# Edge loop of a graph attention layer: bf16 parts at register addresses, selection on VectorE, four message places

## The reference

```
src = randint(100000, 0, 6250); dst = sort((6250 * uniform ** 2))
h = (layernorm(x) @ W.T).reshape(n, 8, 32)
alpha = sum(h[src] * a_src) + sum(h[dst] * a_dst)
alpha += sum(relu(edge_attr @ edge_W.T + edge_b) * h[dst])     # per edge and head
alpha = where(alpha >= 0, alpha, 0.2 * alpha)
attn = softmax of alpha over the edges of one dst
out = segment_sum(h[src] * attn, dst) + bias;  x = x + out
x = x + experts(layernorm(layernorm(x)))                        # router, top 2, gelu
```

## Time and profile before

| | us |
|---|---|
| median of 3 runs (2123.89 to 2133.44) | 2126.27 |
| profiled execution | 2128.02 |
| its span | 2126.0 |
| PE busy | 2009.7 |
| DVE busy | 1515.8 |
| ACT busy | 1352.4 |
| POOL busy | 1181.9 |

### The profile page before, as it was taken

How to read it: one execution, slowest core, us unless ns; L and a number is a source line. 1 busy time by engine, 2 the same in 40 slices (tenths; PEclk the granted TensorE clock), 3 DMA queues, 4 the chain that set the end, 5 groups by cost and what they waited for, 6 DMA issues and landing times. The chain is left out here.

```text
span 2126.0 us, 41064 instructions
## 1 busy us (share of the span) xinstructions
PE 2009.7 (95%) x11612; PEld 1585.9 (75%) x11612; DVE 1515.8 (71%) x3458; ACT 1352.4 (64%) x3892; POOL 1181.9 (56%) x1125
## 2 busy tenths in 40 slices
PE   7799999999999999999999676899999999999997
PEld 6566666766666666666666434899999999999996
DVE  7289999999999999999999897544444444444442
ACT  4698888988988988988988565433333333333332
POOL 1377777776776766666666000355555555555553
PEclk9899999999999999999999887999999999999998
DMA  9766565555555555555554688222222222222221
GB/s 252 227 194 175 170 186 175 172 179 165 169 176 163 167 170 163 158 168 160 157 165 143 230 267 190 46 39 36 38 39 36 38 38 36 38 38 36 38 38 23
DMA packets 160559, 270.94 MB, mean 127 GB/s; under 512 B 36239, under 2 KB 114864, under 8 KB 160211
## 3 DMA queue, kind: packets, MB, share of 16 engines
q0 software_dynamic: 61920, 139.45, 27.6%
q1 hardware_dynamic: 89706, 121.22, 18.6%
q10 hardware_dynamic: 8712, 7.65, 1.1%
HBM read 231.06 MB, written 37.17 MB: 126 GB/s over the span
## 5 line engine op out<-in xcount | busy, mean ns | idle before, releaser
L679 POOL DMA_INDIRECT arena<-h_tab,src x784 | 759.6, 969 | 375.6 <-issue 211.8
L1687 ACT ACTIVATE arena<-psum,arena 128x128 f32<-128x128 f32 x840 | 240.1, 368 | 518.2 <-PE psum L1637 518.2
L881 PE MATMUL psum<-arena 128*128 128x256 f32 x1760 | 479.1, 395 | 9.9 <-DVE arena L973 8.0
L902 PE MATMUL psum<-arena 128*128 128x264 f32 x1760 | 475.0, 393 | 2.5 <-DVE arena L996 2.4
L1637 PEld LDWEIGHTS psum<-arena 128*128 128x128 f32 x3360 | 392.9, 192 | 7.5 <-issue 2.2
L902 PEld LDWEIGHTS psum<-arena 128*128 128x128 f32 x1760 | 320.4, 190 | 100.3 <-issue 50.8
L1637 PE MATMUL psum<-arena 128*128 128x128 f32 x3360 | 393.4, 276 | 1.8 <-DVE arena L1709 1.8
L881 PEld LDWEIGHTS psum<-arena 128*128 128x128 f32 x1760 | 318.8, 191 | 98.2 <-issue 42.5
L1653 PE MATMUL psum<-arena 128*128 x1680 | 379.8, 379 | 0.0
L1599 POOL DMA_INDIRECT out_rows<-arena,src x105 | 208.3, 1984 | 247.2 <-DVE arena L1722 244.2
L1653 PEld LDWEIGHTS psum<-arena 128*128 128x128 f32 x1680 | 311.1, 190 | 38.0
(11 more groups left out here) (233 smaller groups left out, 1917.9 us busy)
## 6 DMA issues: line engine op xcount, KB each, us to landing
arena<-rel_list SPq DMA_DIRECT2D x110, 512.0 KB
arena<-in_W SPq DMA_DIRECT2D x16, 1024.0 KB, 12.3
arena<-h_tab,src POOLq DMA_INDIRECT x784
arena<-ea_slots SPq DMA_DIRECT2D x440, 27.0 KB
arena<-in_x SPq DMA_DIRECT2D x12, 896.0 KB, 8.5
h_tab<-arena SPq DMA_DIRECT2D x6, 952.0 KB, 7.9
out_rows<-arena SPq DMA_DIRECT2D x5, 896.0 KB, 5.4
xn<-arena ACTq DMA_DIRECT2D x5, 896.0 KB, 6.9
```

The source lines that it names most:

```text
L679: pool.indirect_dma_start(rows[:, (p % RING * U + k) * TW:(p % RING * U + k + 1) * TW], None, d.h_tab[:, :], bass.IndirectOffsetOnAxis(ap= ...
L881: last = nc.tensor.matmul(ps[:, HDT + x, y * UE:(y + 1) * UE], hj[:, (s // 2 * 2 + y) % HJ, x * P:(x + 1) * P], oht[:, half % OT, (u + y) ...
L902: last = nc.tensor.matmul(ps[:, AGG + a % 2, 0:HS], oh[:, a % OH, k, :], msg[:, a % MSG, k, :], start=(k == 0), stop=(k == U - 1))
L1687: last = nc.scalar.activation(hT[:, b, h * P:(h + 1) * P], ps[:, UP + 2 * b + half, h % 4 * P:(h % 4 + 1) * P], ACT.Gelu, bias=b1_now[:, b ...
```

## The change

- `expand` multiplies in bf16: h of every node tile is kept in three bf16 parts that add up to the fp32 value (`PARTS` = 3), and PE takes its weights at a register address from there. The one-hot targets become bf16 (`d.rel`, `oht`). `node_rows` on ACT and its ring `hj` are gone.
- The parts are made in `prepare`: POOL for groups 0 to 5, four operations each, after its list gathers; DVE for group 6, in steps 2 to 5 of the loop. h itself passes through three stage buffers, and the sums of a node tile lie over parts that have been used: `acc` shares the arena with them. ACT clears two tiles' places at a time, four times a round, behind the expansion (`clear_ahead`), in place of all at the start.
- DVE makes all selections.
- `MSG` is 4.
- Arena addresses move. W1 is loaded in halves: four at the loop's end, five in `attend`, seven in `route`; all of W2 is loaded in `attend`, three experts at its start and the others behind the groups whose sums are used up.

Core of the diff (the arena's bookkeeping and the moved loads are left out):

```diff
-RING, RENC, HJ, OH, OT, EB, MSG = 18, 5, 4, 4, 3, 3, 2
+RING, RENC, OH, OT, EB, MSG = 18, 5, 4, 3, 3, 4
...
+            for i in range(GROUPS - 1):                      # prepare, POOL
+                h, rest, first, second, third = parts_of(c, i)
+                pool.wait_ge(h_copied, (i + 1) * GT + 2)
+                nc.gpsimd.tensor_copy(first, h).then_inc(cast, 1)
+                pool.wait_ge(cast, 4 * i + 1)
+                nc.gpsimd.tensor_tensor(rest, h, first, ALU.subtract).then_inc(cast, 1)
+                pool.wait_ge(cast, 4 * i + 2)
+                nc.gpsimd.tensor_copy(second, rest).then_inc(cast, 1)
+                pool.wait_ge(cast, 4 * i + 3)
+                nc.gpsimd.tensor_tensor(third, rest, second, ALU.subtract).then_inc(cast, 1)
...
                 if k == 0:                                   # prepare, ACT take_h
                     act.wait_ge(rs_made, i + 1)
+                    if i >= 3:
+                        act.wait_ge(rows_stored[i - 3], 32)
+                        act.wait_ge(cast, 4 * (i - 3) + 2)
...
-        by_scalar = lambda g: g >= SELECTED and g % 4 == 3
-        by_vector = lambda g: g + 1 - max(0, (g - 3) // 4)
+        by_vector = lambda g: g + 1
...
-            def node_rows(s, js):
-
-                if s >= HJ:
-                    act.wait_ge(hd_done, (s - HJ) // 2 * 2 + 2)
-                h_j = h_all[:, ds(js[s % CS] * TW, TW)].rearrange("p (h f) -> p h f", f=FW)[:, :, 1:D + 1]
-                nc.scalar.copy(hj[:, s % HJ, :].rearrange("p (h f) -> p h f", h=H), h_j).then_inc(hj_made, 1)
...
+            def clear_ahead(j, k):
 
                 if k == 0:
+                    act.wait_ge(split, 4)
+                two = acc[:, ds((j + 2 * k + 1) * ST, 2 * ST)].rearrange("p (b n) -> p b n", b=2)[:, :, 0:HS]
+                nc.scalar.activation(two, c.ones[:, 0:1].unsqueeze(2).to_broadcast([P, 2, HS]), ACT.Copy, scale=0.0).then_inc(cleared, 1)
...
                 if x == 0:                                   # PE, expand
-                    if by_scalar(s // 2):
-                        pe.wait_ge(oht_squared, 2 * (s // 8))
-                    else:
-                        pe.wait_ge(oht_made, by_vector(s // 2))
-                    pe.wait_ge(hj_made, s + 2)
+                    pe.wait_ge(oht_made, by_vector(s // 2))
                 if s >= 2:
                     pe.wait_ge(prod_made, s - 1)
                 for y in range(2):
-                    last = nc.tensor.matmul(ps[:, HDT + x, y * UE:(y + 1) * UE], hj[:, (s // 2 * 2 + y) % HJ, x * P:(x + 1) * P],
-                                            oht[:, half % OT, (u + y) * UE:(u + y + 1) * UE], start=True, stop=True)
+                    j = js[(s // 2 * 2 + y) % CS]
+                    for q in range(PARTS):
+                        last = nc.tensor.matmul(ps[:, HDT + x, y * UE:(y + 1) * UE], parts[:, ds(j * (PARTS * IN) + (q * IN + x * P), P)],
+                                                oht[:, half % OT, (u + y) * UE:(u + y + 1) * UE], start=(q == 0), stop=(q == PARTS - 1))
...
+                if 2 <= t < 6:                               # DVE
+                    part(t - 2)
```

More of the change, by code:

```diff
@@ L104, with parts_of @@
     pass
+def parts_of(c, i):
+    h = c.stage[i % 3].rearrange("p (k h f) -> p k h f", h=H, f=FW)[:, :, :, 1:D + 1]
+    rest = c.arena[:, LISTS:LISTS + REST_WORDS].rearrange("p (k h f) -> p k h f", k=GT, h=H)
+    group = c.arena[:, PARTS_AT + i * GT * ST:PARTS_AT + (i + 1) * GT * ST].bitcast(BF16).rearrange("p (k q h f) -> p k q h f", k=GT, q=PARTS, h=H)
+    return (h, rest, *(group[:, :, q] for q in range(PARTS)))
 def semaphores(nc, ctx, *names):
@@ L146, in take @@
                 return c.arena[rows, self.at - n:self.at]
-        work, lists = Region(H_AT + J * TW, ACC_AT), Region(ACC_AT, REST_AT)
+        lists, early = Region(0, LISTS), Region(LISTS, REST_AT)
         row = slice(0, 1)
-        h_all = c.h_all
-        x_all = work.take(J * IN)
-        w_nat = work.take(KH * IN).rearrange("p (k i) -> p k i", k=KH)
+        x_all = c.arena[:, X_AT:REST_AT]
+        w_nat = early.take(KH * IN).rearrange("p (k i) -> p k i", k=KH)
+        below = early.take(PAIRS)
+        hi_tile, iota_t, val_row = (early.take(PAIRS, row) for _ in range(3))
+        assert early.at >= LISTS + REST_WORDS
+        work, late = Region(early.at, ACC_AT), Region(ACC_AT, PARTS_AT)
+        two_stages = work.take(2 * GT * TW)
+        c.stage = [late.take(GT * TW), two_stages[:, 0:GT * TW], two_stages[:, GT * TW:]]
         a_bd = work.take(KH * 2 * H).rearrange("p (k h) -> p k h", k=KH)
@@ L163, in prepare @@
         xT = work.take(3 * IN).rearrange("p (b i) -> p b i", b=3)
-        hi_row, hi_tile, iota_t, val_row, last_i = (work.take(PAIRS, row) for _ in range(5))
+        hi_row, last_i = (work.take(PAIRS, row) for _ in range(2))
         p_int, p_by32, p_by8 = (work.take(1) for _ in range(3))
@@ L851, in _ @@
                     exponent(ch)
-                if 3 <= t < 3 + CS:
-                    clear_sums(t - 3)
+                if t % CS == 0 and 0 < t <= SLOTS:
+                    (j_first,) = load_words(nc, c.slots[0:1, t - CS:t - CS + 1], mybir.EngineType.Activation, 0, J - 1)
+                if t % 2 and CS < t < SLOTS + CS:
+                    if t == CS + 1:
+                        act.wait_ge(split, 4)
+                        nc.scalar.activation(acc[:, 0:HS], c.ones[:, 0:1].to_broadcast([P, HS]), ACT.Copy, scale=0.0).then_inc(cleared, 1)
+                    if t % CS == 1:
+                        act.wait_ge(hd_done, t - CS - 1)
+                    clear_ahead(j_first, t % CS // 2)
         @block.tensor
@@ L1065, in _, with part @@
             nc.vector.tensor_scalar(c.ends, c.ends, -0.5, 2 * BIG, ALU.add, ALU.mult).then_inc(ends_listed, 1)
-            dve.wait_ge(cleared, 3)
+            dve.wait_ge(marked, 3)
+            def part(n):
+                h, rest, first, second, third = parts_of(c, GROUPS - 1)
+                if n:
+                    dve.wait_ge(split, n)
+                if n == 0:
+                    last = nc.vector.tensor_copy(first, h)
+                elif n == 1:
+                    last = nc.vector.tensor_tensor(rest, h, first, ALU.subtract)
+                elif n == 2:
+                    last = nc.vector.tensor_copy(second, rest)
+                else:
+                    last = nc.vector.tensor_tensor(third, rest, second, ALU.subtract)
+                last.then_inc(split, 1)
             for t in range(STEPS):
@@ L1134, in attend @@
         LAST = len(TILES)
+        AFTER_MEAN = {1: (3,), 2: (4, 5), 3: (6,), 4: (7,)}
+        assert all(W2_AT + (e + 1) * (HID // P) * IN <= ACC_AT + FIRST[i + 1] * ST for i, es in AFTER_MEAN.items() for e in es)
         bank = lambda n: n % 3
@@ L1168, in _ @@
                     load(i - 1 + XB)
+                for e in AFTER_MEAN.get(i, ()):
+                    sp.wait_ge(mean_made, i + 1)
+                    second_weights(e)
             for b in range(XB):
```

194 lines of the change are left out of this document (98 added, 96 removed).

## The result

The changed kernel takes 2122.45 us (median of 12 runs, 2117.04 to 2125.76), the kernel before, on the same chip, 2126.91 us (12 runs, 2123.89 to 2134.01): ratio 0.9972, 95% interval 0.996 to 0.9984. So it is faster by 4.5 us, 0.2%, where 20 us were forecast. The profiled execution has a span of 2121.2 us against 2126.0.

The account below looks back on a forecast made before the run. PE was taken to bound the steady loop (2.457 of 2.479 us a step), DVE just behind, POOL full in the first third. Loop -28 and late start +8 gave -20: 2107 us from a median of 2126.3, range 2080 to 2148.

Parts of the forecast that it names:

- Expansion 0.11 a matmul: Edge loop, PE: six bf16 matmuls a step at 0.11 us each, 0.66 in all, 0.20 less a step, PE at 2.26.
- The wait for aggregation gone: Edge loop, DVE: four message places remove the once-a-round wait of messages for an aggregation, 18.6 us or 0.077 a step.
- Step 2.39: Edge loop: DVE at 2.39 us a step, above PE's 2.26, in place of 2.479; 28 us gained from step 142 to 460.
- The head's slack: Loop's head: the four DVE split operations in steps 2 to 5, up to 2 us each, lie under the first gathers.
- the reserve: POOL's 8 us lead at step 142; it repays 8 of the 16 us late start, leaving 8 lost.
- B: Rival, edge loop: the sequencer bounds PE through six register-addressed weight loads a step; at 0.15 us each 2163 us; chance 0.15.
- C: Rival, edge loop: bf16 weight loads show, six matmuls take 0.82 us, step about 2.45, total 2126 us; chance 0.22.
- D: Rival, prologue: POOL's split operations cost only 6.2 us a group, gathers still start at 84, total 2092 us; chance 0.19.
- POOL then ends at 99.5: Prologue: POOL's splits of h take 10.9 us a group, 65.4 from 34.1; loop starts near 100 in place of 81.3.
- Group 5 is ready at 72.3, so it isn't waiting that sets this end: Prologue: h of group 5 is there at 72.3 us, before POOL's end at 99.5, so POOL's own work sets that end.
- free by a hair: Prologue, stage buffers: group 3's second operation ends at 72.3 us, just before ACT starts group 6 at 72.95.
- Attend at 0, with an end at +5: Attend stage: loading 10.5 MB of weights in place of 2 barely fits and costs 0, at most 5 us; DVE bounds it.

Follow-up runs that it names:

- e2: Changed kernel plus range asserts (2199.1 us), with GpSimd pausing after group 0 until VectorE's prologue list work is done: 2202.6 us, 1.035 of the kernel before.
- e3: Changed kernel plus range asserts (2199.1 us), with GpSimd making three casts of h per group, no subtractions: 2184.4 us, 1.0263 of the kernel before.
- e4: Changed kernel plus range asserts (2199.1 us), splits of groups 0 to 5 moved from GpSimd to ScalarE and VectorE, group 0 stored early: 2204.0 us, 1.035.
- e7: Changed kernel with 16-bit list reading (2152.2 us); GpSimd splits only groups 0 to 3, VectorE the rest in the loop; second cuts late, group 0 stored early: 2153.2 us.
- e6: Changed kernel plus range asserts (2199.1 us), with W2 loads of experts 3 to 7 moved from attend to routing: 2198.4 us, 1.0312 of the kernel before.
- e8: Changed kernel with 16-bit list reading (2152.2 us), groups 4 to 6 split in the loop and W2 loads moved to routing: 2146.0 us, 1.007.
- e18: Changed kernel with 32-bit lists, maxima, GpSimd asserts, early ScalarE reading (2134.2 us), plus mended prologue and W2 loads in routing: 2114.9 us, 0.9942 of the kernel before.
- e5: Changed kernel with the two lists that waits compare against read as 16-bit halves, stride two, no assert: 2152.2 us, 1.0104 of the kernel before.

## Why the prediction was wrong

- **The loop's pace was right.** Expansion 0.11 a matmul: six in 0.82 us. Selection 0.35: 0.363. The wait for aggregation gone: yes, with 8.2 of 18.6 us back at the sums. Step 2.39: 2.362, VectorE busy 96%. The loop stage lost 49 us, 10 more than forecast: 36.0 for 28 between step 142 and the last product, and 3.5 at the end for nothing. The head's slack was right too. The first gather came 33.5 us later and step 142's product 25.9, so 7.6 were repaid from the reserve where the forecast had 8, though step 142 itself stood at 440.1 before and not at the 433 that counting from 81.3 gave (the first product came at 92.0). Rivals B and C fell: PE is idle 29 us of 600, and D with them (10.7 us a group, not 6.2). That the time, 2122, lies nearest to C's 2126 is chance.
- **The step that failed: "POOL then ends at 99.5", in the splitting of h.** The two durations were right where VectorE left POOL alone (1.68 and 3.5 to 3.6 for 1.55 and 3.9, 10.7 us a group for 10.9). Wrong was that they lay beside VectorE at no cost to it or to themselves. Taking POOL's work away restored VectorE's durations (e2), halving it took 16 us off the first gather (e3), and without it no operation was stretched (e4). In the changed kernel the list work up to the first `without_first` ran from 56.2 to 80.1 us, before from 47.6 to 52.7; ACT stood 18.1 us, POOL 11.4, and POOL ended at 115.4. The 16 us over 99.5 are these 11.4 and some 6 by which POOL's own operations were stretched, less 1, since six groups at 10.7 are 64.3 and not 65.4. Prologue +35.3 for +19. The Trainium skill states this ("SBUF — State Buffer", "SBUF: two separate sides"): VectorE and GpSimd share a port pair, and whichever starts first holds it for its whole instruction, against VectorE operations with two SBUF inputs or in a 2-port mode. The trace agrees: 0.15 us became 3.52. I had priced GpSimd's operations and not asked what runs beside them.
- **"Group 5 is ready at 72.3, so it isn't waiting that sets this end"** came from the kernel before, whose ACT didn't depend on a stretched VectorE. It was ready at 101, and group 4, for which POOL did wait, at 90.8 (before 62.1).
- **The store of group 0.** I had followed the cast that frees a stage place ("free by a hair"), not the store, which SyncE issues behind the slot lists: 7.3 us of ACT, and the same pattern again in e7 with group 3. It lies ahead of the 18.1 us and started the list work 8.6 us later; no run takes it away alone, so its share isn't separated. An estimate from the rows: with list work as short as before, ACT would have gone on from 62.9 and group 4 been ready at about 73, before POOL's 79.5, store or no store; with the store early and the list work stretched, group 4 would still have come some 3 to 4 us after POOL.
- **Attend at 0, with an end at +5:** +8.8. The loads fit by volume, but x waited behind them: 9.4 us of wait for 2.0. e6, e8 and e18 took half of the wait away.

Put together: -20 forecast, -10 for the faster loop, +16 for the prologue, +9 for attend, is -5; measured -4.8 between the spans.

## What to carry to other kernels

Work put on an idle GpSimd isn't free beside VectorE's: read VectorE's timeline under it for two-input operations, and move the split to a time when VectorE waits anyway or in the loop's head, shared with ScalarE. When a change gives buffers a second reader or fewer places, follow each release back to the queue that issues it, and put stores ahead of waits they don't need. Where an engine is at 96%, a stall of 1.1 us per round on its neighbour cost next to nothing here and one of 2.3 us half a microsecond a round (e5): small register work is worth pricing by a run.

## What the runs showed of the hardware

- A VectorE operation with two SBUF inputs that meets a GpSimd cast or subtraction of 1792 elements waits until that one ends: 128x4 compare 0.15 to 3.52 us, 128x7 addition 0.17 to 2.96, and casts from fp32 too (128x1024, 0.69 to 3.90; 128x256, 0.28 to 1.76). Statistics of 7 tiles (2.38 us) and memsets kept their time beside it. It goes the other way too: GpSimd's subtraction took 4.4 us for 3.5 where a VectorE operation of 128x1024 had begun first.
- GpSimd needs 1.68 us for a cast of 128x1792 fp32 to bf16 and 3.5 to 3.6 us for a subtraction; VectorE 2.0 for either, ScalarE 1.68 for the cast.
- Reading 16 words into ScalarE's registers stopped it 1.1 us; as 8 words of 32 bits and 8 of 16 bits 2.27 us; with a range assert on eight of them 2.95.
- Register-addressed bf16 weight loads and 256-column matmuls followed each other at 0.11 us, with a register instruction ahead of each.
